# Late loads, two more heads of maxima at the entry, and values ahead of the maxima's scores in an attention block with a mixture of experts

## What is computed

```python
x = x + xattn(layernorm(x), ctx, ctx)        # 8 batches x 256 tokens x 512
x = x + ffn(layernorm(x))                     # mixture of experts, 32 experts, top 4
# xattn: 32 query heads of 16, 8 key/value groups
q, k, v = x @ Wq.T, ctx @ Wk.T, ctx @ Wv.T
attn = softmax(q @ k.T / 4)                   # per head, 256 x 256
out = (attn @ v) @ Wfc.T + bfc
# ffn: routing, then for each chosen expert silu(x @ Wg) * (x @ Wu) @ Wd,
# and 0.05 times a smaller expert shared by two
```

## Time and profile before

| what | value |
|---|---|
| median of 3 runs | 1131.07 us (1130.87 to 1133.53) |
| the profiled execution's own time | 1135.69 us |
| its span | 1133.9 us |
| attention, by the trace | 0 to about 426 us |
| route | about 426 to 511 us |
| experts | from about 511 us to the end |
| PE busy in the span | 1032.1 us, 91% |
| DVE busy | 418.6 us, 37% |

### The profile page before, as it was taken

The page is one execution under the profiler, slowest core; times in us unless marked ns, Lnnn a source line. Parts: engine busy times, 40 slices in busy tenths (PEclk is TensorE's granted clock), DMA queues, the critical chain, the costliest instruction groups (busy, mean ns, idle before and its releaser), DMA issues.

```text
span 1133.9 us, 19012 instructions
## 1 busy us (share of the span) xinstructions
PE 1032.1 (91%) x5518; PEld 664.7 (59%) x5520; DVE 418.6 (37%) x1039; ACT 349.3 (31%) x643; POOL 297.2 (26%) x387
## 2 busy tenths in 40 slices
PE   7689999999998979427999999999999999999995
PEld 6556666666665437215666666666665666666662
DVE  4476667766666524691111111111111111111110
ACT  2245454454545533141222222222222222222221
POOL 2101101011020000202344334334333344433432
PEclk9799999999999998757999999999999999999998
DMA  6433032130320003922765675675666667667443
GB/s 206 151 90 71 21 90 57 34 71 21 90 57 16 2 1 134 378 103 47 218 151 141 215 224 143 212 224 146 189 171 148 207 162 209 189 171 219 73 67 56
DMA packets 51449, 146.65 MB, mean 129 GB/s; under 512 B 9552, under 2 KB 18896, under 8 KB 47056
## 3 DMA queue, kind: packets, MB, share of 16 engines
q1 hardware_dynamic: 32192, 99.43, 26.3%
q0 software_dynamic: 17632, 42.74, 19.4%
q10 hardware_dynamic: 1584, 3.93, 1.0%
HBM read 100.73 MB, written 29.36 MB: 115 GB/s over the span
## 4 chain that ended last, share of the span: by engine, by line
PE 53%; issue 0%; DMA 0%; POOL 0%; ACT 0%; DVE 0%; POOLq 0%; ACTq 0%
PE y_ps L1420 18%; PE g_ps L1403 15%; PE u_ps L1403 15%; PE xt_ps L1396 3%; PE at_ps L1412 2%; DMA xg<-xd,gidx 0%; POOL out_x L1307 0%; ACT yb L1339 0%; ACT xT L1328 0%; DVE aT L1361 0%; ACT sg L1332 0%; DVE a L1374 0%; DVE a L1375 0%; POOL gidx L1290 0%; ACTq L1338 0%
## 5 line engine op out<-in xcount | busy, mean ns | idle before, releaser
L1420 PE MATMUL y_ps<-W,aT 128*128 x468 | 215.6, 597 | 1.1 <-DVE aT L1361 0.8
L1307 POOL DMA_INDIRECT out_x<-yb,yidx x78 | 125.3, 1606 | 297.2 <-DMA out_x<-yb,yidx 134.9
L348 ACT ACTIVATE pt<-stp 128x512 f32<-128x512 f32 x256 | 139.2, 597 | 169.4 <-PE stp L638 169.4
L470 DVE TENSOR_REDUCE mx<-s 128x2 f32<-128x512 f32 x256 | 163.0, 681 | 63.7 <-PE s L624 63.5
L1403 PE MATMUL g_ps<-W,xT 128*128 x624 | 183.3, 437 | 0.9 <-ACT xT L1328 0.9
L1403 PE MATMUL u_ps<-W,xT 128*128 x624 | 181.3, 434 | 0.0
L1403 PEld LDWEIGHTS u_ps<-W,xT 128*128 128x128 f32 x624 | 119.1, 191 | 49.9 <-issue 0.8
L1403 PEld LDWEIGHTS g_ps<-W,xT 128*128 128x128 f32 x624 | 113.5, 192 | 39.0 <-issue 2.4
L1374 DVE TENSOR_TENSOR a<-u_ps,sg 128x192 f32<-128x192 f32 x78 | 27.9, 358 | 291.5 <-ACT sg L1332 291.5
L1420 PEld LDWEIGHTS y_ps<-W,aT 128*128 128x128 f32 x468 | 83.5, 192 | 77.4 <-issue 77.3
L1332 ACT ACTIVATE sg<-g_ps 128x320 f32<-128x320 f32 x78 | 34.1, 437 | 306.2 <-PE u_ps L1403 306.2
(11 more groups left out here) (172 smaller groups left out, 949.5 us busy)
## 6 DMA issues: line engine op xcount, KB each, us to landing
W<-in_wts SPq DMA_DIRECT2D x32, 2048.0 KB, 8.2
qst<-q SPq DMA_DIRECT2D x42, 256.0 KB, 4.9
ctxT<-in_ctx SPq DMA_DIRECT2D x8, 512.0 KB, 3.5
xd<-r_xn SPq DMA_DIRECT2D x16, 256.0 KB, 2.0
out_x<-xs SPq DMA_DIRECT2D x1, 4096.0 KB, 13.9
kst<-k SPq DMA_DIRECT2D x48, 64.0 KB, 2.1
xs<-in_x ACTq DMA_DIRECT2D x1, 2560.0 KB, 11.2
qst<-nm SPq DMA_DIRECT2D x128, 2.0 KB
```

What stands on the lines that cost most here:

```text
L348: act.activation(pt[g % 2][:, 2 * (j % 2) + r, :, :], stp[n % STP][:, :, :], ACT.Exp, scale=DH ** -0.5).then_inc(exp_done, 1)
L470: dve.tensor_reduce(mx[j // CH % 2][:, h:2 * G:G], s1[r][:, :, :], AX.X, ALU.max)\
L1307: pool.indirect_dma_start(out[:, :], bass.IndirectOffsetOnAxis(yidx[p][:, :], 0), yb[p][:, :], None, compute_op=ALU.add).then_inc(y_added, ...
L1420: m = pe.matmul(y_ps[:, :], aT[p][:, c, :], W[:, bass.ds(buf, 1), GW + c * D:GW + (c + 1) * D].rearrange("p a d -> p (a d)"), start=(c == ...
```

## The change

Four edits. `X_BEGINS` now has a group for every batch. SP issues the groups for batches 3 to 7 in step 0 of batches 0 to 4, behind the stacking of k, and in batch 0 Wfc and Bfc behind them; ACT issues none. Before the loop PE and DVE make the maxima of steps 4 and 5 of batch 0 too (`ENTRY` = 6), and the first four steps make those of steps 6 to 11 (`EARLY`); on DVE the moments of batch 2 move behind them. In each even step PE does `values`, then `late_items`, then the maxima's scores.

```diff
-X_BEGINS = (0, 2, 4, 6)
+X_BEGINS = tuple(range(0, NT, TT))
+ENTRY = 6
+EARLY = ((6,), (7, 8), (9, 10), (11,))
+VALUES_FIRST = tuple(range(0, J, 2))
...
-            if b == 0 and j < LEAD - CH:
-                return [(0, CH + 2 * j), (0, CH + 2 * j + 1)]
+            if b == 0 and j < len(EARLY):
+                return [(0, m) for m in EARLY[j]]
...
                     if j == 0 and b < NB - 1:
                         for n in range(3):
                             stack_k(b + 1, n)
+                    if j == 0 and b + 3 < NB:
+                        load_x(b + 3)
+                    if j == 0 and b == 0:
+                        sp.dma_start(Wfc[:, :, :], wfc).then_inc(w_loaded, DMA)
+                        sp.dma_start(Bfc[:, :], bfc).then_inc(w_loaded, DMA)
...
-            act.dma_start(xs[:, X_BEGINS[3]:NT, :], xv[:, X_BEGINS[3]:NT, :]).then_inc(x_loaded[3], DMA)
-            act.dma_start(Wfc[:, :, :], wfc).then_inc(w_loaded, DMA)
-            act.dma_start(Bfc[:, :], bfc).then_inc(w_loaded, DMA)
...
             split_max(0)
+            q_split(1, 0)
+            for j in range(CH, ENTRY):
+                row_max(0, j)
             moments(2)
-            q_split(1, 0)
...
             project_q(1, 0, range(C // 2, 2 * C))
+            for j in range(CH, ENTRY):
+                scores_for_max(0, j)
             pe.wait_ge(kst_ready, 1)
...
                     side_items(b, j)
-                    for b1, j1 in maxima_of(b, j):
-                        scores_for_max(b1, j1)
-                    late_items(b, j)
+                    if j not in VALUES_FIRST:
+                        for b1, j1 in maxima_of(b, j):
+                            scores_for_max(b1, j1)
                     if j == 0 and b:
                         values(b - 1, G - 1)
                     elif j and j % 2 == 0:
                         values(b, j // 2 - 1)
+                    late_items(b, j)
+                    if j in VALUES_FIRST:
+                        for b1, j1 in maxima_of(b, j):
+                            scores_for_max(b1, j1)
```

## The result

| | before | changed |
|---|---|---|
| median | 1131.03 us (7 runs, 1130.36 to 1133.53) | 1138.14 us (7 runs, 1135.84 to 1142.46) |
| profiled execution, its span | 1135.69, 1133.9 us | 1137.78, 1136.0 us |
| mean granted clock of the profiled execution | 0.961 | 0.951 |
| first transposes of the route stage on PE, the end of attention | 427.90 us | 432.92 us |

The changed kernel is slower, by a ratio of 1.0068 (95% interval 1.0048 to 1.0088), some 7 us. Runs over 1.5% above the fastest of the same kernel count as slow and stay out of every ratio; it is one run, of the changed kernel measured again. 1122.7 was forecast, within 1112 to 1135. The profiled execution of before was 4.7 us above its median, so the spans show less of the difference than the times.

What follows compares the result with a forecast made beforehand. PE was taken as the bound, busy 91% of the span, with attention waits on DVE to recover. Terms 0 + 1.2 + 2.8 + 5.9 - 1.5 = 8.4 us less took the median from 1131.07 to 1122.7, range 1112 to 1135.

Steps and rivals of the forecast that it cites:

- The likeliest case: Whole kernel: faster by more than 0.3% or 3.4 us, chance 0.71.
- Values first, 2.8 us a batch: PE's even steps: values ahead of maxima's scores remove buffer waits, gaining 2.8 us in a batch without other changes.
- still within: Batches 1 to 5: step 10's weighing on DVE, 0.7 us more before its row maxima, still covered by side items.
- the wait for `ov`: Step 6: values wait 0.3 us for ACT to empty ov; hidden in batches 1 to 4 by the late loads.
- Batches 6 and 7, 5.9 us: Last attention batches, few side items: 9.6 us of waits removed, 3.7 us remaining, a gain of 5.9 us.
- The load of x, 11.2 us: Batches 1 to 4: late rows delay DVE's moments in step 4 and PE in step 5, costing 11.2 us in all.
- D - 1.42: Cost in us, per batch, of x rows landing D late for DVE: 3.4, 3.2, 2.3 and 2.3 in batches 1 to 4.
- The clock, 1.5 us: PE's waits of 3 us in batches 1 and 2 may lower the clock; 1.5 us allowed in all.
- the clock falls in every one of these waits: Rival, PE's waits for late rows: four times 3 us of clock loss instead of 1.5, giving 1133; chance 0.10.
- Batch 0 at 0 us: Entry and batch 0: earlier first scores offset by an idle of some 8 us; between 4 lost and 3 won.
- Wfc, Bfc cost nothing: Batch 0: issuing these loads late was taken as free, since their first users are in batch 1.
- The rival of late landing: Rival, x loads: each us of landing beyond 3.4 costs 1 us in five batches; 1138 at 6.5 us; chance 0.17.

Runs made afterwards that it cites:

- filled: Changed kernel plus unread identity transposes on PE in step 5's wait, batches 0 to 4 (60 in batch 0, 20 in others): 1133.42 us, ratio 1.0016 to before.
- the reordering alone: Kernel before with only PE's new order (values and late items ahead of maxima's scores in even steps): 1113.02 us, ratio 0.9841; again 1115.13 us.
- moments in step 7: Changed kernel with DVE's moments of batch b + 3 in step 7 of batch b instead of step 4: 1116.11 us, ratio 0.9867 to before.
- loads one batch earlier: Changed kernel with SP issuing each group of x one batch earlier, Wfc and Bfc still late: 1115.50 us, ratio 0.9856 to before.
- Wfc and Bfc later: Changed kernel with x loads one batch earlier, and Wfc, Bfc issued in step 8 of batch 0 instead of step 0: 1111.51 us, ratio 0.9823 to before.
- the late loads alone: Kernel before with x loads, Wfc and Bfc issued by SP behind the stacking of k, none on ACT: 1151.85 us, ratio 1.0173 to before.

## Why the prediction was wrong

The likeliest case was "faster", and the time came out above the upper end of the range. Attention was to be 8.4 us shorter and is 5.0 longer in the two profiles, 13.4 us apart. **The step that failed is the price of the clock: 1.5 us allowed "in all", where the changed kernel's profile shows some 8.** The rest of the miss is three terms with the right mechanism and the wrong size, 2 to 3 us each.

That the clock's price can be read rests on one small sum. Where the clock is 1.00, a batch with a load takes 43.32 us and DVE's wait for its rows, as far as the traces have it; the price of the clock is what a batch takes beyond that:

| run, batch | DVE's wait | 43.32 + wait | measured | beyond |
|---|---|---|---|---|
| changed, 1 (clock 1.00) | 4.45 | 47.77 | 47.77 | 0 |
| changed, 2 | 5.25 | 48.57 | 50.17 | 1.60 |
| changed, 3 | 4.70 | 48.02 | 49.38 | 1.36 |
| changed, 4 | 5.18 | 48.50 | 50.06 | 1.56 |
| filled, 1 (clock 1.00) | 3.72 | 47.04 | 47.03 | 0 |
| filled, 2 (clock 1.00) | 4.02 | 47.34 | 47.43 | 0.1 |
| filled, 3 (clock 1.00) | 5.07 | 48.39 | 48.40 | 0 |
| filled, 4 | 5.98 | 49.30 | 50.87 | 1.57 |

The constant is taken from the first line; the three filled batches at full clock then come out within 0.1 us.

Each term against what was measured:

- **Values first, 2.8 us a batch: right, a little large.** Batch 5 takes 44.50 us in the changed kernel (44.6 was forecast), a gain of 2.87. Batches 1 to 4 of the reordering alone save 2.43 each. For the missing 0.4 a place stands out that the text held to be "still within", step 11: in the changed kernel its maxima's scores wait (228.20 to 229.04, 0.84 us instead of 0.44), since DVE adds the output and weighs the values of step 10 ahead of that step's row maxima, and these now come later on PE. Batches 1 to 4 were to gain 12.4 us with the wait for `ov` hidden; by the sum above they gain 10.5 (4 x 47.37, less 4 x (43.32 + 1.42)).
- **Batches 6 and 7, 5.9 us: mis-sized.** From step 1 of batch 6 to the last transpose of maxima the reordering alone saves 2.9 us (59.25 against 56.36), and the changed kernel 3.0. Two of the waits that stay were priced too low. In step 11 of batch 6 PE comes from the step's scores to its maxima's scores in 1.69 us where 0.44 would do, and loses 0.38 more inside them, 1.6 us in all instead of 1.1; in step 1 of batch 7 it is 0.82 instead of 0.11, and 0.38 more, 1.1 us instead of 0.54. The rest of the 3 us was not traced.
- **The load of x, 11.2 us: the mechanism right, the size too small.** DVE waits and PE idles in the steps foretold. DVE's waits in batches 1 to 4 are 19.6 us in all, against 16.8 forecast, which by D - 1.42 makes 13.9 us instead of 11.2. The landing was 3.6 to 3.9 us, not 3.4. What was off more is SP: the stacking of k was taken at 3.83 us in batches 3 and 4; in the changed kernel it takes 4.46, 4.94, 4.64 and 4.96 us in batches 1 to 4.
- **The clock, 1.5 us: the step that failed.** Batches 2 to 4 lost 4.5 us to it in the one profile. In the other of the same kernel it fell behind all four waits, and the same sum gives 9.8. At the end of attention 3.9 us more went (35.71 us where profiles at full clock have 31.75 to 31.87), a place that the prediction did not price at all: PE's wait ahead of step 12 of batch 7 and the gaps in the output projection. Together that is 8.4 us in the profile of the changed kernel. Filling the waits took 4.7 us back, and not all of the falls. This was the rival *the clock falls in every one of these waits*, given 0.10 and 1133. The argument against it, that "2 to 3 us of idle is half of the entry's", took a shorter idle for a harmless one: waits of 2.8 to 3.4 us were enough in batches 2 to 4.
- **Batch 0 at 0 us: right, in part by luck.** The first scores start at 36.74 us (39 was forecast, 41.88 before); the transpose of chunk 1's maxima at 51.27 (forecast 52); the rows land at 66.96, the maxima's scores of step 5 start at 69.10 after 7.59 us of waiting, for 70.5 and 8. It comes out 0.85 us ahead, of an execution of the kernel before that lay 4.7 us above its median; how much of this is the change is open.
- **"Wfc, Bfc cost nothing": true only behind a larger wait.** The text looked at their users, not at the third chunk's maxima, which SP issues behind them. In the changed kernel DVE's wait for the rows covers it. With the rows in time, these two loads cost PE some 3 us (4.8 us of waiting with them, 1.7 without).

What carries the verdict is shown twice. Take the wait away in either of two ways, later moments or earlier loads, and 22 to 23 us come back; the net change of attention then is near the gain of the reordering. How much of the loss is idle and how much clock differs from execution to execution: 4.5 and 9.8 us of clock in batches 1 to 4 of the two profiles, 4.7 us by the times with the waits filled. The rival of late landing had the right direction and the right place; at 3.6 to 3.9 us it was not its mechanism that decided here. A landing of 5.7 us, in batch 4 of the kernel with the waits filled, shows that it can come.

"Issue the DMA early, do compute, wait on its semaphore late", as the Trainium skill has it (DMA: Bandwidth & Descriptors, Rules for kernel authors): the trace agrees, with a price of 22 us, lower clock included, for rows that come 4 to 5 us too late, and once 9.5. The fit of the Trainium skill for one transfer (same page, Anatomy of one DMA), from which the prediction had its estimate of 3.2 us for 512 KB, is for another issue path; here it was 3.6 to 3.9 us in batches 1 to 4 of the changed kernel.

## What to carry to other kernels

A transfer moved to a later place must be held against the first instruction that waits for it and against everything queued behind that on its engine; here moving the wait by three steps, or the load by one batch, turned 0.7% slower into 1.3 or 1.4% faster. Price an idle of TensorE with the clock behind it: the loss shows as longer matmuls with no wait beside them, and work that nobody needs, put into the wait, tells how much of it is the clock, if the waits themselves stay as they were: compare them in both traces. And put no large load ahead of a small transfer that the critical engine waits for.

## What the hardware showed that I had not expected

- Short waits of TensorE can be followed by the lower clock, and whether they are differs from one execution to the next. One wait stands in ten of the profiles, ahead of the scores of step 12 in batch 7, with 1.91 to 1.96 us each time: in seven the clock is lower right behind it, in three (moments in step 7, loads one batch earlier, Wfc and Bfc later) it is 1.00. In the kernel before and the late loads alone the wait is 1.49 and 1.53 us, and the clock is 1.00. In batch 1 the changed kernel had waits of 2.58 us, with the clock at 1.00 behind it, and in the other execution 3.03 us, with a fall. With the mean granted clock between 0.959 and 0.948, eleven runs of this one program spread over 1129 to 1144 us, where 17 of the kernel before in the same group have 1130 to 1139.
- Six transfers of k took SP between 3.82 and 4.96 us to issue, in the same kernel, and the loads of x do not explain it. In the changed kernel batches 0 to 4, which carry a load, take 4.08 to 4.96 us, and batches 5 and 6, which carry none, 3.82. But with the waits filled batches 1 to 4 carry the same loads and take 3.82 or 3.83, and in the kernel before, where no batch carries one, batches 0 to 2 take 4.76, 4.95 and 4.73. The cause stays open.
